# Last sums of a decoder's output: ScalarE scales and stores each block, TensorE adds four ranks, GpSimd two

## The chip, the core and the metric

The kernel runs on one NeuronCore of a Trainium2 chip. The core has five engines with instruction streams of their own, that meet only at semaphores: TensorE (PE in the profile, its weight loads PEld), VectorE (DVE), ScalarE (ACT), GpSimd (POOL) and SyncE (SP), which here only issues DMAs. ScalarE and GpSimd can issue DMAs too. TensorE reads SBUF and writes the eight banks of PSUM; GpSimd does not reach PSUM. The metric is device microseconds of one execution.

## The reference, cut to what matters

Two decoder layers run over 2048 tokens of width 256, each with an attention-like part, a cross attention and a feed-forward part, and a layer norm after each. The change touches only the very last step: the sum of the routed experts' results of a token with what it already has, and the last norm.

```
def _layernorm(x, axis=-1, eps=1e-05):
    m = jnp.mean(x, axis=axis, keepdims=True)
    v = jnp.var(x, axis=axis, keepdims=True)
    return (x - m) / jnp.sqrt(v + eps)
...
    routed = jnp.einsum('te,teh->th', cw, eo)      # six chosen experts of 32 per token
    shared = jax.nn.silu(x @ shared_w_gate) * (x @ shared_w_up) @ shared_w_down
...
    out = routed + shared + ANCHOR_ALPHA * anchor
...
    x = _layernorm(x + _L1_ffn_ref(x, ...), axis=-1)
    return x
```

## The kernel before

All tensors are float32. One large SBUF tensor, `arena`, holds everything; the names in the code are slices of it, and the profile writes "arena" for each of them. The last stage is written by hand, engine by engine, in `tensor_experts`, `scalar_experts`, `vector_experts`, `gpsimd_experts` and `sync_experts`. It has two loops.

The first (`steps_g`) runs over 158 tiles of 128 sorted rows, for 31 of which the anchor experts and for 127 the routed experts are applied. GpSimd scatters each result to its place in the DRAM tensor `yr`, in which the six results of a token stand in a row. VectorE meanwhile adds the anchor results to X.

The second (`steps_i`) is the one in question. It runs over 16 blocks of 128 tokens. SyncE waits for the last scatters and then issues 16 loads (L2221), one per block, each of 128 x 1536 values (768 KB): six ranks of 256 columns per token, into `WB`. Then, in the same queue, come 16 stores (L2224), each behind a wait until its block is scaled. A step n of `steps_i` is "weigh" for block n, "sum" for block n-1 and "scale" for block n-2; an engine takes from this order what belongs to it:

- TensorE, at "weigh": waits for the load of block c and adds ranks 0, 1, 2 by three matmuls with the identity matrix into bank c % 4 (L142 is the line of the helper `mm`). The bank must be free, that is, read by VectorE for block c-4.
- GpSimd, at "weigh": adds ranks 3 and 4 into `tmp3[c % 2]` (L2168). At "sum": (variance + eps) to the power -0.5, 128x1 (L180, in the helper `norm_rstd`).
- VectorE, at "sum": adds rank 5 to X (L2142), then tmp3 (L2145), then the bank (L2148), then the statistics (L167, L170) and the variance (L172). At "scale" for the block before: waits for L180 and for the store that used the same buffer of `xt2_ring` three blocks ago (`o_out`), and writes (x - mean) * rstd there (L187).
- ScalarE does nothing in this loop.

The helper that scales, and the end of SyncE's program:

```
        def norm_scale(v, n, nb, src, dst):
            st = stats[n % 6]
            v.wait_ge(rstd, n + 1)
            for b in range(nb):
                h = v.tensor_scalar(dst(b), src(b), st[:, 24 + 2 * b:25 + 2 * b], st[:, 40 + b:41 + b], ALU.subtract, ALU.mult)
```

`stats` is a ring of six tiles: a block's mean is in column 24, its variance in 32, its rstd in 40.

Of the kernel before, what the change touches and what calls it, by code (L numbers as in the profile page):

```python
# [64 lines left out]
def build(nc, ins, out):  # L65
    with ExitStack() as ctx:
# [1880 lines left out]
        def vector_ends(v, u):  # L1947
# [57 lines left out]
        y2_out = [(s_, 64) for s_ in yg_in]  # L2005
        ag_land = [sem(f"ag_land{i}") for i in range(4)]
        o_out = [sem(f"o_out{i}") for i in range(3)]
        w_copied, silu_done, an_added, added, paired, out_done, tiled, ranked = (
            sem(n) for n in ("w_copied", "silu_done", "an_added", "added", "paired", "out_done", "tiled", "ranked"))
        blocks_in = [(s_, 16) for s_ in x_in + w_in] + [(s_, 64 if i == 0 else 48) for i, s_ in enumerate(taps_in)] + [(s_, 32) for s_ in ctx_in]  # L2010

        def wait_block(e, n):
# [18 lines left out]
        def steps_i():  # L2031
            for n in range(18):
                for u, d in (("weigh", 0), ("sum", 1), ("scale", 2)):
                    if 0 <= n - d < 16:
                        yield u, n - d

        def tensor_experts(t):
            for u, n in steps_g():
# [30 lines left out]
            for u, c in steps_i():  # L2069
                if u == "weigh":  # L2070
                    t.wait_ge(blocks_in[c][0], blocks_in[c][1] + 16)
                    b, k = use(("sum", c), c % 4)
                    t.wait_ge(bank_free[b], k)
                    for kk in range(3):
                        h = mm(t, banks[b][:, 0:256], ident, WB[:, c * 1536 + kk * 256:c * 1536 + kk * 256 + 256], kk == 0, kk == 2)
                    h.then_inc(bank_full[b], 1)

        def scalar_experts(a):
            a.wait_ge(tiled, 1)
            for u, n in steps_g():  # L2080
                I = 64 if n < NTA else 128
                if u == "wl" and n % 2:
                    load_anchor(a, n)
                elif u == "tr" and I == 128:
                    if n >= 3:
                        b, k = U["gu", n - 3]
                        a.wait_ge(bank_full[b], k + 1)
                    b, k = U["tr1", n]
                    a.wait_ge(bank_full[b], k + 1)
                    a.activation(xt2_ring[n % 3], banks[b][:, 0:256], ACT.Copy).then_inc(bank_free[b], 1)  # L2090
                elif u == "gu":
                    if n >= 3:
                        b, k = U["dn", n - 3]
                        a.wait_ge(bank_full[b], k + 1)
                    b, k = U["gu", n]
                    a.wait_ge(bank_full[b], k + 1)
                    a.activation(h2_ring[n % 3][0:I, 0:128], banks[b][0:I, 0:128], ACT.Silu).then_inc(silu_done, 1)  # L2097
                elif u == "dn":
                    if n >= NY:
                        wait_result(a, n - NY)  # L2100
                    b, k = U["dn", n]
                    a.wait_ge(bank_full[b], k + 1)
                    a.activation(y2_ring[n % NY], banks[b][:, 0:256], ACT.Copy, scale=x2_ring[n % NX][:, 257:258]).then_inc(bank_free[b], 1)  # L2103

        def vector_experts(v):
            for u, n in steps_g():
# [30 lines left out]
            for u, c in steps_i():  # L2137
                xx = xblock(c)
                if u == "sum":
                    b, k = U["sum", c]  # L2140
                    v.wait_ge(blocks_in[c][0], blocks_in[c][1] + 16)
                    v.tensor_tensor(xx, WB[:, c * 1536 + 1280:c * 1536 + 1536], xx, ALU.add).then_inc(added, 1)  # L2142
                    v.wait_ge(added, 3 * c + 1)
                    v.wait_ge(paired, c + 1)
                    v.tensor_tensor(xx, tmp3[c % 2], xx, ALU.add).then_inc(added, 1)  # L2145
                    v.wait_ge(added, 3 * c + 2)
                    v.wait_ge(bank_full[b], k + 1)
                    v.tensor_tensor(xx, banks[b][:, 0:256], xx, ALU.add).then_inc(bank_free[b], 1)  # L2148
                    v.wait_ge(bank_free[b], k + 1)
                    held[c] = norm_stats(v, 1, lambda i: xx)  # L2150
                    v.engine_nop().then_inc(added, 1)
                elif u == "scale":
                    if c >= 3:
                        v.wait_ge(o_out[c % 3], 16 * (c // 3))
                    norm_scale(v, held[c], 1, lambda i: xx, lambda i: xt2_ring[c % 3]).then_inc(out_done, 1)

        def gpsimd_experts(p):
            for u, n in steps_g():
# [4 lines left out]
            for u, c in steps_i():  # L2163
                if u == "weigh":
                    if c >= 2:
                        p.wait_ge(added, 3 * (c - 2) + 2)
                    p.wait_ge(blocks_in[c][0], blocks_in[c][1] + 16)
                    p.tensor_tensor(tmp3[c % 2], WB[:, c * 1536 + 768:c * 1536 + 1024], WB[:, c * 1536 + 1024:c * 1536 + 1280], ALU.add).then_inc(paired, 1)  # L2168
                elif u == "sum":
                    norm_rstd(p, 1)  # L2170

# [8 lines left out]
        def sync_experts(s):  # L2180
# [38 lines left out]
            s.wait_ge(w_copied, NT1)  # L2219
            for c in range(16):  # L2220
                s.dma_start(WB[:, c * 1536:(c + 1) * 1536], yr[c * 768:(c + 1) * 768, :].rearrange("(p k) f -> p (k f)", k=6)).then_inc(blocks_in[c][0], 16)  # L2221
            for c in range(16):
                s.wait_ge(out_done, c + 1)
                s.dma_start(out[c * 128:(c + 1) * 128, :], xt2_ring[c % 3]).then_inc(o_out[c % 3], 16)  # L2224
            for j in range(3):
                s.wait_ge(o_out[j], 16 * len(range(j, 16, 3)))

# [158 lines left out]
```

## Time and profile before

| | us |
|---|---|
| median of 3 runs (lowest, highest) | 1797.25 (1795.85, 1801.81) |
| the profiled execution | 1799.82 |
| its span, first to last instruction | 1797.9 |
| the last scatter issued by GpSimd | 1730.1 |
| first and last of the 16 loads issued | 1732.3, 1744.3 |
| last scaling (L187) begins | 1793.5 |

### The profile page before, as it was taken

The page shows a single profiled execution, that of the slowest core. Times are in us where ns is not written, and L with a number is a line of the kernel's source. Part 1 is how long each engine was busy: PE and PEld are TensorE (multiplying, and loading weights), DVE is VectorE, ACT ScalarE, POOL GpSimd, SP SyncE. Part 2 cuts the span into 40 slices and gives each one's busy share as a digit, 9 for nine tenths or more (in the row PEclk, how much of TensorE's full clock was granted, in tenths as well). Part 3 has the DMA queues.
Part 4 walks back from the last instruction along what each step waited for, and adds up shares of the span by engine and source line. Part 5 has one row for each costly group of instructions (what it writes and reads, how often), then busy time and mean ns, then how long its engine had stood idle before and what let it go on. Part 6 is the DMA issues. An engine that isn't in the chain of part 4 may idle for free.

```text
span 1797.9 us, 29185 instructions
## 1 busy us (share of the span) xinstructions
PE 1498.5 (83%) x10012; PEld 1132.1 (63%) x10012; DVE 924.0 (51%) x2506; ACT 538.5 (30%) x1375; POOL 506.9 (28%) x505
## 2 busy tenths in 40 slices
PE   7668987399999998359997798888876799999972
PEld 3455766289999997135674466565653467888862
DVE  7363555511121112897753457585776222666655
ACT  4204443112222221001111254343441112666630
POOL 2020100111111102432222111343344522665653
PEclk9999998599999998679999899999987855999987
DMA  7860000298989982100000511122346664555543
GB/s 211 219 219 25 1 26 13 79 395 326 323 326 329 332 320 83 50 24 0 1 1 1 167 53 42 53 83 83 104 135 223 216 200 143 169 167 158 155 190 150
DMA packets 135088, 260.48 MB, mean 145 GB/s; under 512 B 13727, under 2 KB 107835, under 8 KB 128672
## 3 DMA queue, kind: packets, MB, share of 16 engines
q1 hardware_dynamic: 116032, 214.82, 35.6%
q0 software_dynamic: 16752, 39.88, 6.4%
q10 hardware_dynamic: 2160, 3.93, 0.7%
q8 instruction: 82, 1.34, 0.3%
q14 instruction: 62, 0.51, 0.1%
HBM read 197.31 MB, written 52.59 MB: 139 GB/s over the span
## 4 chain that ended last, share of the span: by engine, by line
PE 51%; DVE 12%; issue 8%; POOL 5%; DMA 3%; ACT 1%; SPq 0%; POOLq 0%; DVEq 0%; ACTq 0%
PE bank L142 47%; POOL xe L1544 3%; PE bank L2045 2%; DVE arena L167 1%; DVE arena L187 1%; DMA out_x<-arena 1%; DMA arena<-xe 1%; DVE arena L1362 1%; POOL arena L1270 1%; DVE arena L1823 1%; POOL arena L180 1%; PE bank L1052 1%; DVE arena L1813 1%; DMA arena<-xd,arena 0%; DVE arena L170 0%
## 5 line engine op out<-in xcount | busy, mean ns | idle before, releaser
L142 PE MATMUL bank<-arena 128*128 128x128 f32 (+9 forms) x8686 | 1351.1, 341 | 181.5 <-issue 25.5
L142 PEld LDWEIGHTS bank<-arena 128*128 128x128 f32 (+5 forms) x8686 | 990.3, 183 | 495.1 <-issue 323.0
L2162 POOL DMA_INDIRECT yr<-arena x158 | 160.0, 1013 | 157.3 <-ACT arena L2103 98.7
L180 POOL TENSOR_TENSOR arena<-arena 128x1 f32<-128x1 f32 (+1 forms) x64 | 54.4, 851 | 521.1 <-DVE arena L172 521.0
L1085 DVE TENSOR_SCALAR arena<-bank,arena 128x128 f32<-128x128 f32 x188 | 52.9, 344 | 272.3 <-PE bank L142 272.3
L1104 POOL DMA_INDIRECT arena<-xd,arena x47 | 44.6, 950 | 295.1 <-PE bank L1052 261.2
L1544 POOL DMA_INDIRECT xe<-arena x112 | 112.4, 1003 | 47.2 <-issue 31.0
L2123 DVE COPY arena<-arena 128x768 f32 x127 | 71.6, 564 | 64.9 <-issue 64.9
L2103 ACT ACTIVATE arena<-bank,arena 128x256 f32<-128x256 f32 x158 | 75.0, 474 | 54.1 <-PE bank L142 48.0
L1725 ACT ACTIVATE arena<-bank,arena 128x256 f32<-128x256 f32 x128 | 59.0, 473 | 98.4 <-DVE arena L1813 98.4
L1072 ACT ACTIVATE arena<-bank,arena 128x128 f32<-128x128 f32 x188 | 53.8, 368 | 90.1 <-PE bank L142 90.1
L2097 ACT ACTIVATE arena<-bank 128x128 f32<-128x128 f32 (+1 forms) x158 | 43.7, 276 | 118.9 <-PE bank L142 118.9
L1063 ACT ACTIVATE arena<-bank 128x256 f32<-128x256 f32 x47 | 18.1, 384 | 201.3 <-PE bank L142 201.3
L2045 PE MATMUL bank<-arena 128*128 128x128 f32 x316 | 69.2, 305 | 9.3 <-DMA arena<-xe 9.2
L187 DVE TENSOR_SCALAR arena<-arena 128x256 f32<-128x256 f32 x160 | 62.0, 438 | 25.3 <-DMA out_x<-arena 14.8
L167 DVE BATCH_NORM_STATS2 arena<-arena 128x6 f32<-128x256 f32 x160 | 58.6, 416 | 2.4
L2131 DVE TENSOR_TENSOR arena<-bank,arena 128x128 f32<-128x128 f32 (+1 forms) x158 | 45.9, 290 | 26.9 <-ACT arena L2097 10.3
L745 DVE TENSOR_REDUCE arena<-bank 128x4 f32<-128x512 f32 x64 | 39.8, 685 | 37.8 <-PE bank L142 37.8
L1251 ACT ACTIVATE arena<-bank 128x512 f32<-128x512 f32 x32 | 19.1, 597 | 123.6 <-PE bank L142 98.1
L1765 POOL TENSOR_TENSOR arena<-arena 128x512 f32<-128x512 f32 x16 | 20.2, 1265 | 118.7 <-DVE arena L1804 118.7
L2045 PEld LDWEIGHTS bank<-arena 128*128 128x128 f32 x316 | 40.9, 153 | 19.3 <-DMA arena<-xe 10.5
L2114 DVE COPY arena<-bank 128x256 f32<-128x256 f32 x31 | 13.2, 424 | 76.3 <-PE bank L2045 76.3
(241 smaller groups left out, 1343.7 us busy)
## 6 DMA issues: line engine op xcount, KB each, us to landing
arena<-in_bank SPq DMA_DIRECT2D x47, 2052.0 KB
arena<-xe SPq DMA_DIRECT2D x158, 129.0 KB, 2.1
arena<-kd SPq DMA_DIRECT2D x16, 1024.0 KB, 11.0
arena<-arena SPq DMA_DIRECT2D x16, 896.0 KB, 4.5
arena<-in_bank SPq DMA_DIRECT2D x8, 1536.0 KB, 11.3
arena<-yr SPq DMA_DIRECT2D x16, 768.0 KB, 14.6
xe<-arena SPq DMA_DIRECT2D x1, 6321.0 KB, 26.1
ys<-arena SPq DMA_DIRECT2D x47, 128.0 KB, 3.2
```

Source lines behind the costliest of these rows:

```text
L142: return t.matmul(o, l, r, start=start, stop=stop, skip_group_check=True)
L167: h = v.bn_stats(st[:, 6 * b:6 * b + 6], src(b)).then_inc(vstep.up(), 1)
L180: p.tensor_tensor(st[:, 40:40 + nb], st[:, 32:32 + nb], cc("mhalf", 0, nb), ALU.pow).then_inc(rstd, 1)
L187: h = v.tensor_scalar(dst(b), src(b), st[:, 24 + 2 * b:25 + 2 * b], st[:, 40 + b:41 + b], ALU.subtract, ALU.mult)
L1072: h = a.activation(h_ring[i % 3][:, m * 128:(m + 1) * 128], banks[b][:, m * 128:(m + 1) * 128], ACT.Relu, bias=sbc(w_ring[i % 5], 4096 + m))
L1085: h = v.tensor_scalar(h_ring[i % 3][:, (4 + m) * 128:(5 + m) * 128], banks[b][:, m * 128:(m + 1) * 128], sbc(w_ring[i % 5], 4100 + m), 0.0 ...
L1544: p.indirect_dma_start(xe, bass.IndirectOffsetOnAxis(ap=posi[i][:, at:at + 1], axis=0), stg[i][:, at * RW:(at + 1) * RW], None).then_inc(a ...
L1725: h = a.activation(f_s[g % 2][:, hh * 512 + j * 256:hh * 512 + j * 256 + 256], banks[b][:, j * 256:j * 256 + 256], ACT.Exp, scale=-1.0, bi ...
L2045: h = t.transpose(banks[b][:, j * 128:(j + 1) * 128], x2_ring[n % NX][:, j * 128:(j + 1) * 128], ident)
L2103: a.activation(y2_ring[n % NY], banks[b][:, 0:256], ACT.Copy, scale=x2_ring[n % NX][:, 257:258]).then_inc(bank_free[b], 1)
L2123: v.tensor_copy(e_ring[n % 4], WB[:, bass.ds(at * ROW1, ROW1)]).then_inc(w_copied, 1)
L2162: p.indirect_dma_start(yr, bass.IndirectOffsetOnAxis(ap=sidx.bitcast(I32)[:, n:n + 1], axis=0), y2_ring[n % NY], None, bounds_check=14335, ...
```

## The change

Four things in the second loop:

1. TensorE adds four ranks (0 to 3) instead of three, and GpSimd adds ranks 4 and 5 instead of 3 and 4. VectorE's addition of the sixth rank (L2142) goes, with its wait for the load.
2. VectorE no longer scales. At "scale" it computes only the shift, -mean * rstd, 128x1.
3. ScalarE scales from X into `xt2_ring` with an Identity activation (scale rstd, bias shift), after waiting for the shift and for the buffer's old store. It waits for its own activation and issues the store from its own queue. SyncE's sixteen stores go.
4. VectorE waits before the statistics of block c until ScalarE has scaled block c-6, whose tile of `stats` they overwrite. One empty instruction per block goes.

```
@@ tensor_experts
-                    for kk in range(3):
-                        h = mm(t, banks[b][:, 0:256], ident, WB[:, c * 1536 + kk * 256:c * 1536 + kk * 256 + 256], kk == 0, kk == 2)
+                    for kk in range(4):
+                        h = mm(t, banks[b][:, 0:256], ident, WB[:, c * 1536 + kk * 256:c * 1536 + kk * 256 + 256], kk == 0, kk == 3)
@@ scalar_experts
+            for c in range(16):
+                st = stats[(NORMS + c) % 6]
+                a.wait_ge(shifted, c + 1)
+                if c >= 3:
+                    a.wait_ge(o_out[c % 3], 16 * (c // 3))
+                a.activation(xt2_ring[c % 3], xblock(c), ACT.Identity, scale=st[:, 40:41], bias=shift[:, c:c + 1]).then_inc(scaled, 1)
+                a.wait_ge(scaled, c + 1)
+                a.dma_start(out[c * 128:(c + 1) * 128, :], xt2_ring[c % 3]).then_inc(o_out[c % 3], 16)
@@ vector_experts, "sum"
-                    v.wait_ge(blocks_in[c][0], blocks_in[c][1] + 16)
-                    v.tensor_tensor(xx, WB[:, c * 1536 + 1280:c * 1536 + 1536], xx, ALU.add).then_inc(added, 1)
-                    v.wait_ge(added, 3 * c + 1)
                     v.wait_ge(paired, c + 1)
                     v.tensor_tensor(xx, tmp3[c % 2], xx, ALU.add).then_inc(added, 1)
-                    v.wait_ge(added, 3 * c + 2)
+                    v.wait_ge(added, c + 1)
                     v.wait_ge(bank_full[b], k + 1)
                     v.tensor_tensor(xx, banks[b][:, 0:256], xx, ALU.add).then_inc(bank_free[b], 1)
                     v.wait_ge(bank_free[b], k + 1)
+                    if c >= 6:
+                        v.wait_ge(scaled, c - 5)
                     held[c] = norm_stats(v, 1, lambda i: xx)
-                    v.engine_nop().then_inc(added, 1)
@@ vector_experts, "scale"
-                    if c >= 3:
-                        v.wait_ge(o_out[c % 3], 16 * (c // 3))
-                    norm_scale(v, held[c], 1, lambda i: xx, lambda i: xt2_ring[c % 3]).then_inc(out_done, 1)
+                    st = stats[held[c] % 6]
+                    v.wait_ge(rstd, held[c] + 1)
+                    v.scalar_tensor_tensor(shift[:, c:c + 1], st[:, 24:25], -1.0, st[:, 40:41], ALU.mult, ALU.mult).then_inc(shifted, 1)
@@ gpsimd_experts, "weigh"
-                    p.tensor_tensor(tmp3[c % 2], WB[:, c * 1536 + 768:c * 1536 + 1024], WB[:, c * 1536 + 1024:c * 1536 + 1280], ALU.add).then_inc(paired, 1)
+                    p.tensor_tensor(tmp3[c % 2], WB[:, c * 1536 + 1024:c * 1536 + 1280], WB[:, c * 1536 + 1280:c * 1536 + 1536], ALU.add).then_inc(paired, 1)
@@ sync_experts
-            for c in range(16):
-                s.wait_ge(out_done, c + 1)
-                s.dma_start(out[c * 128:(c + 1) * 128, :], xt2_ring[c % 3]).then_inc(o_out[c % 3], 16)
```

The order on VectorE in the middle of the second loop, before: the empty instruction (ISA), the scaling of a block (L187), then the six instructions of the next sum.

```order
L2151 ISA
L187 TENSOR_SCALAR arena<-arena 128x256
L2142 TENSOR_TENSOR arena<-arena 128x256
L2145 TENSOR_TENSOR arena<-arena 128x256
L2148 TENSOR_TENSOR arena<-bank,arena 128x256
L167 BN_STATS arena<-arena 128x6
L170 BN_AGGR arena<-arena 128x2
L172 TENSOR_SCALAR arena<-arena 128x1
```

The same place after; L2155 is the line of the old L2145, L2158 that of L2148, L2167 the shift.

```order
L2167 SCALAR_TENSOR_TENSOR arena<-arena 128x1
L2155 TENSOR_TENSOR arena<-arena 128x256
L2158 TENSOR_TENSOR arena<-bank,arena 128x256
L167 BN_STATS arena<-arena 128x6
L170 BN_AGGR arena<-arena 128x2
L172 TENSOR_SCALAR arena<-arena 128x1
```

Of seven working instructions per block five wide or statistic ones stay, and the scaling has become an instruction on one column.

The end of ScalarE's program before, from the last tiles of the first loop (L2097 Silu, L2103 the weighted results) to its last branch:

```order
L2097 ACTIVATE arena<-bank 128x128
L2103 ACTIVATE arena<-bank,arena 128x256
L2097 ACTIVATE arena<-bank 128x128
L2103 ACTIVATE arena<-bank,arena 128x256 x2
L66 UNCONDITIONAL_BRANCH
```

And after (L2101 and L2107 are the same two lines), where the pair L2114, L2116 stands sixteen times:

```order
L2101 ACTIVATE arena<-bank 128x128
L2107 ACTIVATE arena<-bank,arena 128x256 x2
L2114 ACTIVATE arena<-arena 128x256
L2116 DMA out_x<-arena 128x256
L2114 ACTIVATE arena<-arena 128x256
L2116 DMA out_x<-arena 128x256
```

The stores have moved from SyncE's queue, where they stood behind all sixteen loads, to ScalarE's, where each stands behind the scaling of its block. All that comes before the second loop stands as it did on every engine.

## Rows read from the trace of the kernel before

**Rows 1.** VectorE's timeline, one block: start, duration, instruction, [idle before <-releaser]

```profile
1765.42 0.41 DVE L187 TENSOR_SCALAR arena<-arena 128x256 f32<-128x256 f32 x1 [14.85 <-DMA out_x<-arena]
1765.74 0.42 DVE L2142 TENSOR_TENSOR arena<-arena 128x256 f32<-128x256 f32 x1
1766.20 0.42 DVE L2145 TENSOR_TENSOR arena<-arena 128x256 f32<-128x256 f32 x1
1766.66 0.42 DVE L2148 TENSOR_TENSOR arena<-bank,arena 128x256 f32<-128x256 f32 x1
1767.12 0.43 DVE L167 BATCH_NORM_STATS2 arena<-arena 128x6 f32<-128x256 f32 x1
1767.58 0.18 DVE L170 BATCH_NORM_AGGREGATE arena<-arena 128x2 f32<-128x6 f32 x1
1767.80 0.15 DVE L172 TENSOR_SCALAR arena<-arena 128x1 f32<-128x1 f32 x1
1767.88 0.41 DVE L187 TENSOR_SCALAR arena<-arena 128x256 f32<-128x256 f32 x1
```

**Rows 2.** SyncE's issues of loads (last two, all) and stores: ns min/median/max, landing

```profile
L2221 SPq DMA_DIRECT2D arena<-yr x2: 1578/1578/1579, 1742.7 to 1744.3; - x2
DMA to landing us min/median/max: 20.5/20.6/20.7
...
L2221 SPq DMA_DIRECT2D arena<-yr x16: 331/450/3646, 1732.3 to 1744.3; - x16
...
L2224 SPq DMA_DIRECT2D out_x<-arena x16: 332/332/1604, 1745.9 to 1793.9; - x16
...
DMA to landing us min/median/max: 1.7/1.7/19.5
```

**Rows 3.** Windows: length, busy and (count) per engine, PEclk, DMA share, GB/s

```profile
1450.00:1460.00 10.00, 10.00 (x35) 6.57 (x34) 1.94 (x7) 2.24 (x6) 2.88 (x3) 0.50 0.47 135
...
1746.00:1748.00 2.00, 1.56 (x6) 1.06 (x6) 1.83 (x6) 0.00 (x0) 1.37 (x2) 1.00 1.01 418
...
1774.00:1775.00 1.00, 0.37 (x2) 0.38 (x3) 0.90 (x4) 0.00 (x0) 0.60 (x1) 1.00 0.39 131
```

**Rows 4.** Timelines of TensorE's first sums, and VectorE's first read of a bank

```profile
1736.57 3.36 PE L142 MATMUL bank<-arena 128*128 128x256 f32 x7 [8.07 <-DMA arena<-yr]
...
1739.60 0.42 DVE L2148 TENSOR_TENSOR arena<-bank,arena 128x256 f32<-128x256 f32 x1 [1.54 <-PE bank L142]
...
1741.64 2.54 PE L142 MATMUL bank<-arena 128*128 128x256 f32 x11
...
1746.20 1.56 PE L142 MATMUL bank<-arena 128*128 128x256 f32 x6 [0.33 <-DMA arena<-yr]
```

**Rows 5.** Timeline: GpSimd's last pair and last power, VectorE's last scaling

```profile
1788.39 1.00 POOL L2168 TENSOR_TENSOR arena<-arena 128x256 f32<-128x256 f32 x1
...
1792.68 0.67 POOL L180 TENSOR_TENSOR arena<-arena 128x1 f32<-128x1 f32 x1 [1.80 <-DVE arena L172]
...
1793.46 0.41 DVE L187 TENSOR_SCALAR arena<-arena 128x256 f32<-128x256 f32 x1 [0.51 <-POOL arena L180]
```

**Rows 6.** ScalarE: activations (busy, mean ns), its DMA issues: 1400 to 1440, alone

```profile
L2103 ACT ACTIVATE arena<-bank,arena 128x256 f32<-128x256 f32 x158 | 75.0, 474 | 54.1 <-PE bank L142 48.0
...
L339 ACT ACTIVATE arena<-arena 128x512 f32<-128x512 f32 x8 | 4.5, 620 | 0.0
...
L2178 ACTq DMA_DIRECT2D arena<-in_banka x7: 344/345/397, 1400.0 to 1438.4; - x7
...
DMA to landing us min/median/max: 2.9/5.4/8.1
...
DMA to landing us min/median/max: 2.6/2.6/2.6
```

**Rows 7.** SyncE's timeline in the first expert stage: two stores, one tile apart

```profile
404.55 0.33 SPq L1114 DMA_DIRECT2D ys<-arena  x1
...
411.80 0.33 SPq L1114 DMA_DIRECT2D ys<-arena  x1
```

More of the change, by code:

```diff
@@ L2007, in build @@
         o_out = [sem(f"o_out{i}") for i in range(3)]
-        w_copied, silu_done, an_added, added, paired, out_done, tiled, ranked = (
-            sem(n) for n in ("w_copied", "silu_done", "an_added", "added", "paired", "out_done", "tiled", "ranked"))
+        w_copied, silu_done, an_added, added, paired, tiled, ranked = (
+            sem(n) for n in ("w_copied", "silu_done", "an_added", "added", "paired", "tiled", "ranked"))
         blocks_in = [(s_, 16) for s_ in x_in + w_in] + [(s_, 64 if i == 0 else 48) for i, s_ in enumerate(taps_in)] + [(s_, 32) for s_ in ctx_in]
@@ L2035, in steps_i @@
                         yield u, n - d
+        NORMS = 48
+        shift = alloc(16)
+        shifted, scaled = sem("shifted"), sem("scaled")
         def tensor_experts(t):
@@ L2149, in vector_experts @@
                     v.wait_ge(bank_free[b], k + 1)
+                    if c >= 6:
+                        v.wait_ge(scaled, c - 5)
                     held[c] = norm_stats(v, 1, lambda i: xx)
-                    v.engine_nop().then_inc(added, 1)
+                    assert held[c] == NORMS + c
                 elif u == "scale":
-                    if c >= 3:
-                        v.wait_ge(o_out[c % 3], 16 * (c // 3))
-                    norm_scale(v, held[c], 1, lambda i: xx, lambda i: xt2_ring[c % 3]).then_inc(out_done, 1)
+                    st = stats[held[c] % 6]
+                    v.wait_ge(rstd, held[c] + 1)
+                    v.scalar_tensor_tensor(shift[:, c:c + 1], st[:, 24:25], -1.0, st[:, 40:41], ALU.mult, ALU.mult).then_inc(shifted, 1)
         def gpsimd_experts(p):
@@ L2165, in gpsimd_experts @@
                     if c >= 2:
-                        p.wait_ge(added, 3 * (c - 2) + 2)
+                        p.wait_ge(added, c - 1)
                     p.wait_ge(blocks_in[c][0], blocks_in[c][1] + 16)
-                    p.tensor_tensor(tmp3[c % 2], WB[:, c * 1536 + 768:c * 1536 + 1024], WB[:, c * 1536 + 1024:c * 1536 + 1280], ALU.add).then_inc(paired, 1)
+                    p.tensor_tensor(tmp3[c % 2], WB[:, c * 1536 + 1024:c * 1536 + 1280], WB[:, c * 1536 + 1280:c * 1536 + 1536], ALU.add).then_inc(paired, 1)
                 elif u == "sum":
```

## The prediction, made before the changed kernel ran

> **What bounds the kernel now.** I read VectorE's waits in the last 70 us first, then its timeline. One wait stands out: 14.85 us in front of L187, the scaling of a block, for a store to out_x [rows 1]. Nothing else there costs more than two microseconds on the engine that carries the chain. The list of DMA issues says why [rows 2]: the stores were issued on SyncE behind the sixteen loads of WB. The last load was issued at 1744.3 and landed 20.5 us later, at 1764.8; the first store, issued at 1745.9, took 19.5 us and landed at 1765.4, where an undisturbed one takes 1.7. L187 writes into a ring of three buffers, so the scaling of block 3 had to wait for store 0, and with it everything behind it on VectorE.
>
> The windows show the loads as a stream at the limit of the DMA engines: share 1.01 at 418 GB/s [rows 3], and so until 1764, so 768 KB every 1.88 us. After the stall VectorE is the bound: its timeline shows seven working instructions a block without a gap, 1765.42 to 1767.88, 2.46 us each [rows 1]. Eleven sums (blocks 5 to 15) were still to do: 11 x 2.46 = 27.1 us from 1765.7, then 5.1 us of tail. So the end of the kernel has two parts that do not overlap: a stream of loads (to 1764.8) and a backlog on VectorE. The best that a change of this stage can do is to make the sums keep up with the loads, and to end soon after the last one lands.
>
> **The change part by part**, on the profiled execution's clock (its span is 1797.9, the execution 1799.82 us, 2.6 above the median of 1797.25).
>
> *VectorE.* L2142 goes (start to start 0.46 in [rows 1]) and L187 goes (0.33). The new 128x1 instruction is not in this trace; the nearest is L172 with the same shape, 0.15 busy and 0.08 to the next start [rows 1]. I take 0.15, with 0.08 and 0.33 (that of the wide L187) as ends. A block is then 2.46 - 0.46 - 0.33 + 0.15 = 1.82 us (1.75 to 2.0). That is just under the 1.88 us between loads, so VectorE no longer falls behind.
>
> *TensorE.* Four matmuls instead of three. At the granted clock of 1.00 (2.4 GHz) eleven records take 2.54 us, two records to a matmul: (2.54 - 0.38) / 10 = 0.216 per record, 0.43 per matmul [rows 4]. A block of six records takes 1.56 with its tail; the block's turn grows from about 1.40 to 1.83 us. It also stays under 1.88. Block 0 meets the low level: seven records in 3.36 us there, 0.86 per matmul [rows 4], so the first sum reaches VectorE 0.86 later, at 1740.45 instead of 1739.60 [rows 4]. Later blocks absorb this, because four banks let TensorE run ahead and the loads set the pace. At the end the fourth matmul lies on the path once: 0.43.
>
> *GpSimd.* The pair is another pair, at the same 1.00 us [rows 5]; with the 0.67 of the power a block costs it 1.67, under the load. No term.
>
> *ScalarE* idled through this stage. An activation 128x256 cost 0.47 from PSUM [rows 6]; one of double the width from the arena took 0.62. I take 0.47, with 0.35 and 0.62 as ends. It issues the store itself: issuing on its queue cost 0.345 [rows 6]. A turn is about 0.9 us, under 1.88. Identity was already used among the Silus without a table load in between, so I price none. What stands behind the new wait on o_out is only ScalarE's own next block; VectorE follows through the wait on scaled, six blocks behind.
>
> *SyncE* loses sixteen issues that come after its loads. That frees nothing by itself.
>
> *The stores in the middle of the loads.* This is the term that decides. First the cost to the loads: a lone store of 128 KB occupied 0.39 of one microsecond of all engines, at 131 GB/s [rows 3]. The trace has no store beside this stream, so it leaves bounds: nothing at all (if it hides), and 1.1 us. The upper one comes from the first expert stage, where a 2052 KB load of weights, a 128 KB store and a gather share 7.25 us per tile (404.55 to 411.80) [rows 7]; 2052 KB at 418 GB/s are 5.03, and half of the 2.2 left over is 1.1 per small transfer. I take 0.39, since it is the same transfer.
>
> Second, how soon such a store lands. On ScalarE's own queue, 256 KB landed 2.6 us after issue with nothing around it, and in 2.9 to 8.1 us, median 5.4, in the stretch where SyncE's bulk loads were in flight [rows 6]. So it is held up, but not always until the end of the bulk. I take the top of that, 8 us, because here the stream never pauses; 4 and 12 are the ends I carry.
>
> The Trainium skill, DMA: Bandwidth & Descriptors, section Queues, rings and completion order, says that each DMA engine goes round the queues it has work for, one packet at a time; its section Issuing engines are not separate DMA queues says that issuing from several engines at once only saves the issuing time. By the first rule the stores slip in between the loads, which is my case; by the second, read strictly, nothing is gained but issue time, and that is the first rival below. The 8.1 us row lies between the two.
>
> *The sum.* Block 0 is scaled at about 1744.8 (1740.45, then VectorE's 1.3 for it, then block 1's sum, which stands ahead of block 0's shift in the order). With 8 us per store and three buffers, ScalarE hands over three blocks per 8.5 us: block 3 at 1753.3, block 6 at 1761.9, block 9 at 1770.3. VectorE needs block 9's scaling only for block 15, and is there at about the same time, so it does not stall. Seven stores or so have passed before the last load lands: 1764.8 + 7 x 0.39 = 1767.5. After that stores land in 1.7 us again and ScalarE works off blocks 10 to 15 at 0.87 each (0.47 + 0.35 + 0.05): 1770.3 + 6 x 0.87 = 1775.5. Then 0.05 + 1.7 for the last store and 2.3 to close, as now (L187 at 1793.46 [rows 5], stored from 1793.9, landed 1795.6, end 1797.9): **1779.6**.
>
> With stores that land in 4 us, ScalarE is never late, and the path is the other one: twelve stores pass, the last load lands at 1764.8 + 12 x 0.39 = 1769.5; TensorE 2.0 to 1771.5; VectorE 0.46 + 0.46 + 0.22 + 0.15 to 1772.8; GpSimd 0.05 + 0.67 to 1773.5; shift 0.2, ScalarE 0.52, to 1774.2; then the same 4.05: 1778.3. With 12 us: 1781. The three lie close, since a slower store means fewer of them in front of the last load. With the ends of the store's cost: nothing gives 1775, 1.1 us gives 1784 to 1788. Forecast: span 1779.5, 18.4 less, and from the median 1797.25 - 18.4 = **1779 us**.
>
> **The rivals.**
>
> *Stores wait for all loads.* If the engines finish what SyncE has queued before they touch ScalarE's queue, stores 0 to 2 land at about 1765.8, block 3 is scaled at 1766.4, and VectorE, six blocks ahead at most, has stood at block 9. It then has six more sums at 1.82 and the tail: its block 9 is normed at 1767.4, and 1767.4 + 6 x 1.82 + 1.4 + 4.0 = 1784, a time of 1783. For it: the 19.5 us of store 0 [rows 2], and the slow end of [rows 6]. Against: the median of 5.4 in the same row, and those 19.5 us were on one queue. It is still a gain, since VectorE gets to block 9 instead of block 5, at 1.82 per block.
>
> *TensorE stays at 1.2 GHz.* 64 matmuls x 0.86 = 55 us from 1736.6 to 1791.4, then 3.1 for the last block's norm and scaling and 4.0 to the end: 1798.5, a time of 1798, no change. For it: from 1450 to 1460 it was busy for all 10.00 us and still granted 0.50 [rows 3]. Against: on these same matmuls, the clock rose 4.8 us after they began, and stayed at 1.00 with 1.56 busy of 2.00 [rows 3, 4]; now it is busier.
>
> *ScalarE's issue blocks* (the slower side). SyncE's own issue once took 3.65 us and others 1.6 while its loads were queued [rows 2]. ScalarE runs in order: if every one of its issues took 3.65, a turn would be 4.12 and sixteen of them would end at 1744.8 + 65.9 = 1810.7, with 4.0 behind: 1814.7, a time of 1814. It turns into a loss from (1797.9 - 4.0 - 1744.8) / 16 = 3.07 per turn, an issue of 2.6 us. Against: 0.397 was the longest of seven issues on its queue beside bulk loads [rows 6], and after 1768 the queues are empty.
>
> *The moved store changes nothing*, that is, some other wait as long as the old one takes its place, within 0.3%: I see none, and leave it a small chance.
>
> **How the numbers follow.** The forecast (stores land among the loads, 1775 to 1788) 0.78; stores wait for all loads 0.13; TensorE at 1.2 GHz 0.03; issue blocks 0.03; another wait in its place 0.03. A measurement of this kernel can tell about 0.3% (5.4 us) from no change. Faster: 0.78 + 0.13 = 0.91; same 0.06; slower 0.03. The range runs from 1774 (a store costs the loads nothing, landing fast: 1775, less one for the scatter of the runs) to 1787 (1.1 us per store; it takes in the first rival).
>
> **What the profile after would show.** The wait of VectorE on out_x is gone, and none over 3 us has come in its place before block 15. The last load lands at 1767 to 1770. VectorE's blocks are 1.8 us while it works and end before 1773. ScalarE's stores land in 4 to 12 us before 1768 and 1.7 after it. If they all land after 1765, the first rival holds; if TensorE shows 0.50 beyond 1745, the second; if ScalarE's issues are longer than 1 us, the third. The forecast is wrong if a store beside the loads costs them more than 1.1 us, or if VectorE's block is not 1.8.

## The result, and the profile after

| us | before | after |
|---|---|---|
| median of 4 runs each, side by side | 1796.7 (1795.85 to 1801.81) | 1778.5 (1776.0 to 1781.1) |
| ratio, 95% interval | | 0.9893 (0.9867 to 0.9919) |
| span of the profiled execution | 1797.9 | 1778.5 |
| first load of the last stage issued | 1732.3 | 1733.9 |
| from there to the end ("the stage") | 65.6 | 44.6 |

1779 was predicted, from 1774 to 1787. The two executions reached the last stage 1.6 us apart; within it 21 us are gone. Later executions reached it anywhere from 1718.6 to 1731.2, whatever the kernel (the last section shows where that arises), so from here on the measure is the stage: from the issue of the first of the sixteen loads to the last instruction. Two executions of the changed kernel gave 44.6 and 44.2 by it. Each stage below is of one profiled execution. One of seven runs of a kernel below (in place, stores by ScalarE) took 2274.6 us at a mean granted clock of 0.633, and the median given for it leaves that run out.

VectorE's timeline of the kernel after, one block from the middle of the loads (start, duration, instruction); it answers to [rows 1]:

```profile
1752.68 0.15 DVE L2167 SCALAR_TENSOR_TENSOR arena<-arena 128x1 f32<-128x1 f32 x1
1752.75 0.42 DVE L2155 TENSOR_TENSOR arena<-arena 128x256 f32<-128x256 f32 x1
1753.20 0.42 DVE L2158 TENSOR_TENSOR arena<-bank,arena 128x256 f32<-128x256 f32 x1
1753.66 0.43 DVE L167 BATCH_NORM_STATS2 arena<-arena 128x6 f32<-128x256 f32 x1
1754.12 0.18 DVE L170 BATCH_NORM_AGGREGATE arena<-arena 128x2 f32<-128x6 f32 x1
1754.34 0.15 DVE L172 TENSOR_SCALAR arena<-arena 128x1 f32<-128x1 f32 x1
1754.41 0.15 DVE L2167 SCALAR_TENSOR_TENSOR arena<-arena 128x1 f32<-128x1 f32 x1
```

A block takes 1754.41 - 1752.68 = 1.73 us, in the very stretch in which VectorE stood still before. Behind the 2.61 us that it waits for TensorE in block 0, its longest wait in the loop is now 0.94 us, for TensorE in block 1.

ScalarE's timeline after. The three groups are the first blocks, blocks 3 to 6 in the middle of the loads, and the last three:

```profile
1745.96 0.60 ACT L2114 ACTIVATE arena<-arena 128x256 f32<-128x256 f32 x1 [15.34 <-DVE arena L2167]
1746.59 0.36 ACTq L2116 DMA_DIRECT2D out_x<-arena  x1
...
1753.74 0.60 ACT L2114 ACTIVATE arena<-arena 128x256 f32<-128x256 f32 x1 [3.73 <-DMA out_x<-arena]
1754.37 0.34 ACTq L2116 DMA_DIRECT2D out_x<-arena  x1
1755.92 0.60 ACT L2114 ACTIVATE arena<-arena 128x256 f32<-128x256 f32 x1 [1.57 <-DMA out_x<-arena]
...
1761.15 0.60 ACT L2114 ACTIVATE arena<-arena 128x256 f32<-128x256 f32 x1 [2.46 <-DMA out_x<-arena]
...
1773.64 0.60 ACT L2114 ACTIVATE arena<-arena 128x256 f32<-128x256 f32 x1 [0.76 <-DVE arena L2167]
1774.27 0.34 ACTq L2116 DMA_DIRECT2D out_x<-arena  x1
1774.71 0.60 ACT L2114 ACTIVATE arena<-arena 128x256 f32<-128x256 f32 x1 [0.47 <-ACT arena L2114]
1775.34 0.34 ACTq L2116 DMA_DIRECT2D out_x<-arena  x1
1775.78 0.60 ACT L2114 ACTIVATE arena<-arena 128x256 f32<-128x256 f32 x1 [0.47 <-ACT arena L2114]
1776.41 0.34 ACTq L2116 DMA_DIRECT2D out_x<-arena  x1
```

The wait for a store has not gone: it has moved to ScalarE, 14.3 us over seven blocks, where it costs VectorE nothing. It is still on the path: the chain of work that ended last runs over three stores in turn, of 7.5, 6.7 and 6.1 us. Block 3 is scaled at 1753.74, as soon as store 0, issued at 1746.59, has landed 7.1 us later, still in the middle of the loads. At the end ScalarE works off its backlog in turns of 1.07 us.

The landing times of all sixteen stores, and of the last two loads (minimum, median, maximum); they answer to [rows 2]:

```profile
L2116 ACTq DMA_DIRECT2D out_x<-arena x16: 338/338/363, 1746.6 to 1776.4; - x16
...
DMA to landing us min/median/max: 1.7/5.0/8.0
...
L2233 SPq DMA_DIRECT2D arena<-yr x2: 1578/1578/1579, 1744.0 to 1745.6; - x2
...
DMA to landing us min/median/max: 23.0/23.3/23.6
```

The last load landed at 1745.6 + 23.6 = 1769.2, 35.3 us into the stage; before it landed at 1744.3 + 20.7 = 1765.0, 32.7 into it, with no store landed yet. After, seven stores had landed by then and an eighth was on its way: 2.6 / 8 = 0.33 us of delay for each.

The windows after (columns as in [rows 3]): TensorE's clock is at 1.00 from 1744 on, and with loads and stores together the DMA engines stay at their limit, a share of 1.01 to 1.03.

```profile
1742.00:1744.00 2.00, 2.00 (x7) 1.59 (x7) 1.52 (x5) 0.00 (x0) 0.62 (x1) 0.64 1.01 424
1744.00:1746.00 2.00, 2.00 (x11) 1.76 (x10) 1.33 (x6) 0.04 (x1) 0.82 (x3) 1.00 1.03 430
1752.00:1754.00 2.00, 2.00 (x11) 1.75 (x10) 1.86 (x7) 0.26 (x1) 1.70 (x3) 1.00 1.01 411
```

### The profile page after: what moved, and what is told of

Its sections match the earlier page's. It is cut to its first block, busy times and chain, and to the rows that moved or that the text cites. A ratio compares the mean times of both kernels' runs of the same rounds, so it can differ in the third digit from the quotient of the medians.

```text
span 1778.5 us, 29227 instructions
## 1 busy us (share of the span) xinstructions
PE 1505.8 (85%) x10044; PEld 1140.6 (64%) x10044; DVE 912.9 (51%) x2490; ACT 548.1 (31%) x1391; POOL 506.7 (28%) x505
## 3 DMA queue, kind: packets, MB, share of 16 engines
q1 hardware_dynamic: 113728, 212.72, 35.5%
## 4 chain that ended last, share of the span: by engine, by line
PE 48%; DVE 14%; issue 8%; POOL 6%; DMA 3%; ACT 1%; SPq 0%; POOLq 0%; ACTq 0%; DVEq 0%
PE bank L142 44%; POOL xe L1544 3%; PE bank L2049 2%; DVE arena L1362 2%; DVE arena L167 1%; DVE arena L187 1%; DMA out_x<-arena 1%; DMA arena<-xe 1%; DVE arena L1353 1%; POOL arena L1287 1%; POOL arena L1270 1%; POOL arena L180 1%; DVE arena L1823 1%; DVE arena L1342 1%; PE bank L1052 1%
## 5 line engine op out<-in xcount | busy, mean ns | idle before, releaser
L142 PE MATMUL bank<-arena 128*128 128x128 f32 (+7 forms) x8718 | 1357.2, 341 | 163.3 <-issue 25.1
L1104 POOL DMA_INDIRECT arena<-xd,arena x47 | 44.7, 951 | 295.3 <-PE bank L1052 261.5
L2107 ACT ACTIVATE arena<-bank,arena 128x256 f32<-128x256 f32 x158 | 75.0, 474 | 54.2 <-PE bank L142 48.1
L2101 ACT ACTIVATE arena<-bank 128x128 f32<-128x128 f32 (+1 forms) x158 | 43.7, 276 | 118.2 <-PE bank L142 118.2
L745 DVE TENSOR_REDUCE arena<-bank 128x4 f32<-128x512 f32 x64 | 39.7, 684 | 37.7 <-PE bank L142 37.7
L187 DVE TENSOR_SCALAR arena<-arena 128x256 f32<-128x256 f32 x144 | 53.9, 430 | 10.0 <-POOL arena L180 9.6
```

Source lines behind the costliest of these rows:

```text
L142: return t.matmul(o, l, r, start=start, stop=stop, skip_group_check=True)
```

## The experiments

The change is three things at once: shorter sums on VectorE, a scaling that VectorE need not wait for, and stores in a queue of their own. The theory: the stall of 14.85 us came from three buffers together with a store that stood behind all loads, and the shorter sums were worth the rest. The rivals: the queue is everything; the queue is nothing but issue time.

**Part one alone: four ranks.** The kernel before, with only this:

```
-                    for kk in range(3):
+                    for kk in range(4):
...
-                    v.tensor_tensor(xx, WB[:, c * 1536 + 1280:c * 1536 + 1536], xx, ALU.add).then_inc(added, 1)
...
-                    p.tensor_tensor(tmp3[c % 2], WB[:, c * 1536 + 768:c * 1536 + 1024], WB[:, c * 1536 + 1024:c * 1536 + 1280], ALU.add).then_inc(paired, 1)
+                    p.tensor_tensor(tmp3[c % 2], WB[:, c * 1536 + 1024:c * 1536 + 1280], WB[:, c * 1536 + 1280:c * 1536 + 1536], ALU.add).then_inc(paired, 1)
```

> The kernel before with the first part of the change alone: four ranks on TensorE, ranks 4 and 5 on GpSimd, L2142 gone; VectorE still scales and SyncE still stores. My theory: the stall for store 0 stays (VectorE waits until the loads have ended), and then eleven blocks take 2.46 - 0.46 = 2.00 us: stage (first load's issue to the last instruction) 65.5 - 5.1 = 60.4 us. Rival, TensorE's fourth matmul becomes the bound, above all at its lower clock after the stall: 63 to 66. Rival, the shorter sums were the main part of the gain: under 55.

Measured: stage 60.4 us; time 1793.7 against 1798.6, ratio 0.9972 (0.9949 to 0.9995). VectorE's longest wait (instruction, what it waited for; total us, count, longest):

```profile
DVE arena L187 <- DMA out_x<-arena: 15.7, 1, 15.7
```

VectorE's timeline of this kernel behind it:

```profile
1761.60 0.41 DVE L187 TENSOR_SCALAR arena<-arena 128x256 f32<-128x256 f32 x1
1761.92 0.42 DVE L2142 TENSOR_TENSOR arena<-arena 128x256 f32<-128x256 f32 x1
...
1763.60 0.41 DVE L187 TENSOR_SCALAR arena<-arena 128x256 f32<-128x256 f32 x1
```

The stall is there in full, 0.9 longer since VectorE reached it sooner; behind it a block takes 2.00 us. The four ranks alone are worth 5.2 of the 21 us, which is the eleven blocks behind the stall at 0.46 each. TensorE was no bound: behind its first bank (2.6 us) VectorE never waited for it.

**The queue alone.** The kernel before, but the stores are issued by ScalarE:

```
@@ scalar_experts
+            for c in range(16):
+                a.wait_ge(out_done, c + 1)
+                a.dma_start(out[c * 128:(c + 1) * 128, :], xt2_ring[c % 3]).then_inc(o_out[c % 3], 16)
@@ sync_experts
-            for c in range(16):
-                s.wait_ge(out_done, c + 1)
-                s.dma_start(out[c * 128:(c + 1) * 128, :], xt2_ring[c % 3]).then_inc(o_out[c % 3], 16)
```

> The kernel before with one thing changed: the sixteen stores are issued by ScalarE instead of SyncE; VectorE still scales. The last stage is timed from the issue of the first of the sixteen loads to the last instruction: 65.6 us in the kernel before (1732.3 to 1797.9), 44.6 in the changed one (1733.9 to 1778.5). My theory: the stall of 14.85 us goes, but stores among the loads land in 7 to 8 us, as after the change, and VectorE's own scaling now waits for the three buffers: about 2.7 us per block until the loads end, then 2.46. Stage 51 to 54 us, 12 to 14 less than before. Rival, the queue is the whole gain: 44 to 46. Rival, another queue saves only issue time: 64 to 66.

Measured: stage 52.1 us; time 1783.0 against 1796.9, ratio 0.9932 (0.9907 to 0.9957). The size was right, the way to it not quite. VectorE's wait for the buffers:

```profile
DVE arena L187 <- DMA out_x<-arena: 0.5, 1, 0.5
```

The landing times of its sixteen stores:

```profile
DMA to landing us min/median/max: 1.7/5.7/7.5
```

VectorE's timeline of this kernel, the scalings of two blocks in a row:

```profile
1751.21 0.41 DVE L187 TENSOR_SCALAR arena<-arena 128x256 f32<-128x256 f32 x1
...
1753.67 0.41 DVE L187 TENSOR_SCALAR arena<-arena 128x256 f32<-128x256 f32 x1
```

I had expected 2.7 us per block from the buffers; VectorE was held by them for 0.5 us in all, and took its own 2.46 per block. Three blocks of 2.46 are 7.4, just about what a store needs. So the queue alone is worth 13.5 us, and what stays is VectorE's length per block.

**All but the queue.** The changed kernel with the stores back on SyncE:

```
@@ scalar_experts
-                a.wait_ge(scaled, c + 1)
-                a.dma_start(out[c * 128:(c + 1) * 128, :], xt2_ring[c % 3]).then_inc(o_out[c % 3], 16)
@@ sync_experts
+            for c in range(16):
+                s.wait_ge(scaled, c + 1)
+                s.dma_start(out[c * 128:(c + 1) * 128, :], xt2_ring[c % 3]).then_inc(o_out[c % 3], 16)
```

> The changed kernel with its stores back on SyncE's queue, behind the sixteen loads; all else as changed. My theory: stores 0 to 2 land only when the loads have ended (about 33.5 us into the stage), ScalarE is held at block 3 and VectorE at block 9 (it needs the scaling of block 3), then six more blocks at 1.73 and the tail: stage 51 to 52 us, 7 more than the changed kernel and 14 less than before. Rival, ScalarE's own queue gave nothing but issue time: 45. Rival, the queue is the whole gain: 64 to 66.

Measured: stage 50.4 us; time 1781.8 against 1796.9, ratio 0.9925 (0.9902 to 0.9948). Its waits:

```profile
ACT arena L2114 <- DMA out_x<-arena: 19.7, 4, 17.2
...
DVE arena L167 <- ACT arena L2114: 9.1, 1, 9.1
```

This is the first rival of the prediction, built on purpose. ScalarE stands 17.2 us at block 3, and VectorE 9.1 us once, at the statistics of the block that needs that scaling. The stage is 6.0 us longer than with the stores on their own queue. So the queue is worth 13.5 us without the rest and 6.0 with it, since VectorE, six blocks ahead instead of three buffers, is hurt less by the same stall.

**No wait for a buffer, and no store among the loads.** ScalarE scales in place in X, where the block has its own room, and SyncE stores behind its loads:

```
-                if c >= 3:
-                    a.wait_ge(o_out[c % 3], 16 * (c // 3))
-                a.activation(xt2_ring[c % 3], xblock(c), ACT.Identity, scale=st[:, 40:41], bias=shift[:, c:c + 1]).then_inc(scaled, 1)
-                a.wait_ge(scaled, c + 1)
-                a.dma_start(out[c * 128:(c + 1) * 128, :], xt2_ring[c % 3]).then_inc(o_out[c % 3], 16)
+                a.activation(xblock(c), xblock(c), ACT.Identity, scale=st[:, 40:41], bias=shift[:, c:c + 1]).then_inc(scaled, 1)
@@ sync_experts
+            for c in range(16):
+                s.wait_ge(scaled, c + 1)
+                s.dma_start(out[c * 128:(c + 1) * 128, :], xblock(c)).then_inc(o_out[c % 3], 16)
```

> The changed kernel, but ScalarE scales in place in X (sixteen buffers, so no wait for a store), and SyncE issues the stores behind its loads. No store then takes time from a load. My theory: the loads end 32.5 us into the stage, as before the change; TensorE's last block starts at 32.6, GpSimd's last power at 36.1, and the end comes 5.2 after that by GpSimd's closing drain (5.03 us in the kernel before), where the last store alone would allow 39.7: stage 41.3 us, 3.3 less than the changed kernel. Rival, that drain does not set the end: 39.7. Rival, the gain needs the stores on their own queue: 51 or more, as with the stores on SyncE and three buffers.

Measured: stage 41.8 us (median 1775.8 beside 1796.9). It was run a second time beside the changed kernel:

> In-place scaling with the stores on SyncE behind the loads, again: stage 41.8 us, 2.8 less than the changed kernel; time 1775 to 1776 against 1778.5.

> The changed kernel once more, beside the three below: stage (first load's issue to the last instruction) 44.6 us.

Measured there: 41.8 us against 44.2. The very queue that made the stall is the better one as soon as nobody waits for the buffers: it holds the stores back by itself until the loads are through, and the last load landed 33.1 and 33.2 us into the stage, not 35.3 and 35.5. In whole times the two could not be told apart (medians 1774.7 and 1774.4 of six runs each, before 1795.6).

**In place, but stores among the loads.** The changed kernel, scaling in X; the stores stay with ScalarE:

```
-                if c >= 3:
-                    a.wait_ge(o_out[c % 3], 16 * (c // 3))
-                a.activation(xt2_ring[c % 3], xblock(c), ACT.Identity, scale=st[:, 40:41], bias=shift[:, c:c + 1]).then_inc(scaled, 1)
+                a.activation(xblock(c), xblock(c), ACT.Identity, scale=st[:, 40:41], bias=shift[:, c:c + 1]).then_inc(scaled, 1)
...
-                a.dma_start(out[c * 128:(c + 1) * 128, :], xt2_ring[c % 3]).then_inc(o_out[c % 3], 16)
+                a.dma_start(out[c * 128:(c + 1) * 128, :], xblock(c)).then_inc(o_out[c % 3], 16)
```

> The changed kernel with in-place scaling (sixteen buffers), stores still issued by ScalarE among the loads. In the changed kernel the three buffers held ScalarE back to the end (its last scaling 2.5 us after the last shift). My theory: that hold goes, but nine to eleven stores instead of seven now pass ahead of the last load, which lands 0.7 later, and GpSimd's closing drain, 5.2 us after the last power, takes over as the end: stage 44.7 us, no gain. Rival, the three buffers alone are the end: 42 to 43. Rival, the in-place kernel of the last batch got its 41.8 us from the buffers and not from the queue: 41.8 here too.

Measured: stage 44.2 us (median 1777.0 beside 1795.6), no gain over the changed kernel. ScalarE's backlog was shorter (its last activation began 40.2 us into the stage instead of 41.5 in the changed kernel beside it), but the loads ended no sooner, and the last store was no longer the end: it had landed at 1773.1, 1.7 us before the kernel ended. What ended last was GpSimd's closing, as the next experiment shows. It is the pair with the kernel above that tells: the same buffers, another queue, 2.4 us.

**What closes the kernel.** In the kernel before, 2.3 us lie between the landing of the last store and the end. The closing instructions of the queues (L66) of the kernel before (times in ns, minimum, median and maximum, then the start):

```profile
L66 POOLq DRAIN  x1: 5026/5026/5026, 1792.6 to 1792.6; - x1
```

and of the kernel after:

```profile
L66 POOLq DRAIN  x1: 4901/4901/4901, 1772.7 to 1772.7; - x1
```

To test it, the in-place kernel with SyncE's stores, but without GpSimd's last power; VectorE copies the variance in its place, so block 15 is not normed:

```
-                elif u == "sum":
+                elif u == "sum" and c < 15:
                     norm_rstd(p, 1)
@@ vector_experts
+                    if c == 15:
...
+                        v.tensor_scalar(st[:, 40:41], st[:, 32:33], 1.0, None, ALU.mult).then_inc(vstep.up(), 1)
```

> As the in-place kernel with stores on SyncE, but GpSimd leaves out its last power, that of block 15: VectorE copies the variance in its place (block 15 of the output is not normed rightly), so that GpSimd's last work is about 2 us earlier. If GpSimd's closing drain sets the end of the in-place kernel, the stage falls from 41.3 to about 39.3 and is then set by the last store. If the drain is no bound, only the 0.5 us that the copy is shorter than the power are seen, from 39.7 to 39.2.

Measured: stage 39.9 us, 1.9 less; with the drain as no bound only 0.5 was to be had. Then the same without leaving anything out (ROOTS is 14):

```
@@ scalar_experts, before the loop
+            a.activation(early[:, 0:1], cc("ones", 0, 1), ACT.Sqrt)
@@ in the loop, before the scaling of block c
+                if c + 1 >= ROOTS and c + 1 < 16:
+                    s1 = stats[(NORMS + c + 1) % 6]
+                    a.wait_ge(variance, NORMS + c + 2)
+                    a.activation(s1[:, 33:34], s1[:, 32:33], ACT.Sqrt).then_inc(rooted, 1)
@@ vector_experts, "scale"
-                    v.wait_ge(rstd, held[c] + 1)
+                    if c < ROOTS:
+                        v.wait_ge(rstd, held[c] + 1)
+                    else:
+                        v.wait_ge(rooted, c - ROOTS + 1)
+                        v.reciprocal(st[:, 40:41], st[:, 33:34]).then_inc(inverted, 1)
+                        v.wait_ge(inverted, c - ROOTS + 1)
@@ gpsimd_experts
-                elif u == "sum":
+                elif u == "sum" and c < ROOTS:
```

> The in-place kernel with stores on SyncE, in which the last two of the sixteen powers move from GpSimd to ScalarE (square root, with its table loaded while ScalarE is idle) and VectorE (reciprocal). Nothing is left out. GpSimd's last power is then that of block 13 and its last work the pair of block 15. If the closing drain set the end, the stage falls from 41.8 to 39.5 to 40 us (the last store then sets it). If moving work off GpSimd at the end does nothing, 41.5 to 42.

The first activation is there so that the table of the root is loaded while ScalarE is idle: the load stands at 1722.96 in this trace and takes 1.28 us. Measured: stage 40.1 us; median 1772.7 against 1795.6, ratio 0.9887 (0.9848 to 0.9927). The issue of the first load on SyncE's timeline of this kernel:

```profile
1726.21 13.45 SPq L2242 DMA_DIRECT2D arena<-yr  x16
```

Its span is 1766.3 us. The closing drain of its GpSimd:

```profile
L66 POOLq DRAIN  x1: 5687/5687/5687, 1759.4 to 1759.4; - x1
```

The drain now ends at 1765.1, 1.2 us before the end. The last store landed 39.8 us into the stage in the in-place kernel, 39.5 without the last power and 39.7 here, so what shortened the stage by 1.9 and 1.7 us was the drain. It is recorded as 5.7 us here, since the power of block 13 and the pair of block 15 fall into it; it ends 4.3 us behind the end of that pair (1760.79), as it does behind the last power elsewhere. By the stage this version beats both kernels, the changed one by 4.1 us; its whole time lies below the changed one's of the same set (1774.4) by less than the scatter.

**The term in dispute, doubled.** The changed kernel with each block stored twice, once to another tensor:

```
+                a.dma_start(extra[c * 128:(c + 1) * 128, :], xblock(c)).then_inc(x_out, 16)
                 a.dma_start(out[c * 128:(c + 1) * 128, :], xt2_ring[c % 3]).then_inc(o_out[c % 3], 16)
```

> The changed kernel, with every block stored twice: ScalarE first stores the unscaled block to another DRAM tensor, then the scaled one to the output. This doubles the one term in dispute, what a store among the loads costs them. In the changed kernel the last load's data ended 34.6 to 34.8 us into the stage with 8.5 to 8.8 stores in front, against 32.3 with one or two: 0.32 us per store. If the cost is linear and ScalarE's queue gets its turn as before, some 16 to 18 stores pass and the last load ends at 37 to 37.7; the stage is 47 to 49 us (44.4 plus 2.6 for the loads, and up to 2 for the queue of the doubled stores). If the queue takes a fixed share of the engines however much is queued, 34.8 and a stage over 49. If stores beside loads grow dearer (1.1 us each), over 42 and a stage over 51.

Measured: stage 52.1 us, time 1783.5 against 1798.6. The landing times of its stores to the output, to the extra tensor, and of the loads, in this order:

```profile
DMA to landing us min/median/max: 1.8/2.0/13.7
...
DMA to landing us min/median/max: 1.7/1.7/11.9
...
DMA to landing us min/median/max: 4.2/14.8/24.8
```

The expectation's second variant holds, that the queue takes a fixed share. Twice as many stores were ready, but when the last load landed, 35.8 us into the stage (1739.1 + 24.1 - 1727.4; 35.3 and 35.5 with single stores), only nine had landed and a tenth was on its way, where it had been seven and an eighth. What grew is the time that a store waits, up to 13.7 us instead of 8.0. ScalarE, held by its buffers, then had nine blocks to go instead of six, each about 1.5 us instead of 1.07: that, and not the loads, is most of what the stage is longer. From the first landing on the nine came over 18 us, one for each load. The packets of the two queues of the changed kernel in its stage, the loads' first (packets, MB, share of the 16 engines):

```profile
q1 hardware_dynamic: 2304, 12.58, 66.6%
q10 hardware_dynamic: 2304, 2.10, 13.4%
```

A load and a store have the same number of packets. If the engines take as many from one queue as from the other in turn, one store passes per load and costs it the time of its bytes, by my estimate 128 / 768 x 1.88 = 0.31 us, which fits the 0.33 measured; no run varied the packets to test this. The Trainium skill says in DMA: Bandwidth & Descriptors, section Queues, rings and completion order, that the engines go round the queues packet by packet; this agrees. What the Trainium skill says there in section Issuing engines are not separate DMA queues, that issuing from several engines only saves issue time, does not fit the 13.5 us of the queue alone here. Why the first store took 7.1 us with no other store before it stays open.

The stages side by side (us):

| kernel | expected | measured |
|---|---|---|
| before | | 65.6 |
| four ranks alone | 60.4 | 60.4 |
| queue alone | 51 to 54 | 52.1 |
| all but the queue | 51 to 52 | 50.4 |
| changed kernel | 47.2 (1779.5 - 1732.3) | 44.6, 44.2 |
| in place, ScalarE stores | 44.7 | 44.2 |
| in place, SyncE stores | 41.3 | 41.8, 41.8 |
| in place, SyncE stores, last power left out | 39.3 | 39.9 |
| in place, SyncE stores, last two powers as roots | 39.5 to 40 | 40.1 |
| every block stored twice | 47 to 49, or over 49 | 52.1 |

## Why the prediction was right, point by point

- **The bound.** Right: a stream of loads, then a backlog on VectorE, held up by store 0. The two partial kernels show both halves at their size: 13.5 us for the queue, 5.2 for the four ranks. The last load was read a little early: its landing was the 20.7 of [rows 2], not 20.5.
- **VectorE.** 1.82 was forecast for a block, 1.73 measured: the shift costs 0.07 from start to start, the lower end that I had given, as L172 does beside its follower.
- **TensorE.** 0.86 later in block 0: the first read of a bank came 8.11 us into the stage instead of 7.27, 0.84 later. Afterwards VectorE waited for it 0.94 us at most, and in the last blocks TensorE was itself waiting for loads. The rival's sum has a slip: 1736.6 + 55 is 1791.6, not 1791.4.
- **GpSimd.** No term, right, but the price was off: the pair took 0.73, not 1.00 (last section).
- **Landing of the stores.** 8 us taken; 7.1, 7.5 and 8.0 for the first three, 6 to 7 for the next. Of the three values carried, the one from the top of the range of other transfers came nearest.
- **Cost to the loads.** 0.39 taken for each of seven stores, 0.33 measured for each of eight; the last load landed 35.3 us into the stage, where I had it at 1767.5 - 1732.3 = 35.2.
- **ScalarE.** 0.47 for the activation, which took 0.60 from SBUF; a turn was 1.07 instead of 0.87. The row of L339, from the arena, was the nearer one and I had put it at the end of the range. Two errors met here: since the stores landed in 6 to 7 us, the scaling of block 9 ended 35.2 us into the stage, where I had 38.0, but the six turns behind it took 7.3 us instead of 5.2. The last activation ended at 42.5 instead of 43.2.
- **The close.** "2.3 to close, as now" is the step that failed. It was read off the kernel before as if it were a fixed cost behind the last store. It was GpSimd's drain, running beside the store; after the change 0.4 us are left. This term was too large by 1.9.
- **The sum.** The stage lost 21 us, where 18.4 were forecast: 1.9 of the difference come from the close, 0.7 from ScalarE. The medians differ by 18.2; that they match the forecast so closely is luck to the extent of those 2.6 us: the changed kernel's profiled execution reached the stage 1.6 us later, and two executions of that same kernel differ by 13.5 us there (last section).
- **Rivals.** Stores behind all loads: not so, and its price was good: a stage of 51.4 forecast (1783.7 - 1732.3), 50.4 measured where the case was built. TensorE at 1.2 GHz throughout: no, it was granted 1.00 from 1744 on. ScalarE's issues never took more than 0.36 us, while SyncE's still took up to 3.4 beside its own backlog.

## What to carry to other kernels

A store that is queued behind a bulk of loads lands after them; that hurts only through the buffers that wait for it. Before moving it to another queue, ask whether the buffers can be had, since the old queue then keeps the stores out of the loads' way for free. What lies between the last landing and the end of a kernel is not a constant: look for the engine whose closing drain ends last, and see that its last work ends earlier, by giving the last small operation to another engine.

## What the runs showed of the hardware that I had not expected

**GpSimd's closing drain** ended 4.3 us behind the end of GpSimd's last work in all twelve profiled executions, whether that was a power (0.55 to 0.73 us) or, with the last powers moved, the pair. Its record runs from 4.9 to 5.7 us, since it starts before that work ends. It was the last to end in the kernel before and in five of the experiments: the four ranks alone, the queue alone, all but the queue, and both in-place kernels with all powers.

**GpSimd's addition beside VectorE's.** The pair took a median of 997 ns before and 726 after, and 721 in the kernel with four ranks alone. Before:

```profile
L2168 POOL TENSOR_TENSOR arena<-arena x16: 717/997/1002, 1736.6 to 1788.4; 128x256 f32<-128x256 f32 x16
```

After:

```profile
L2180 POOL TENSOR_TENSOR arena<-arena x16: 713/726/728, 1738.1 to 1769.3; 128x256 f32<-128x256 f32 x16
```

Four ranks alone:

```profile
L2165 POOL TENSOR_TENSOR arena<-arena x16: 716/721/727, 1722.9 to 1770.4; 128x256 f32<-128x256 f32 x16
```

Before, it began with an addition of two SBUF tensors on VectorE (1768.67 beside L2145 at 1768.66) and was 0.28 longer: in twelve of the sixteen blocks it began so and took 0.996 to 1.002 us, in the other four 0.717 to 0.722. In block 0 the pair was the first, at 1736.60, and VectorE's addition of two SBUF tensors came 0.02 us behind it; there the pair took 0.72, and the addition 0.98 instead of 0.42:

```profile
1736.62 0.98 DVE L2142 TENSOR_TENSOR arena<-arena 128x256 f32<-128x256 f32 x1 [8.87 <-DMA arena<-yr]
```

So of the two that began together, the later one was delayed. The Trainium skill, SBUF — State Buffer, section Who interferes with whom, says that such a VectorE instruction and a GpSimd instruction that reads SBUF hold each other up; the rows agree, though no run was made for this alone.

**The time ahead of the stage.** The two executions of the changed kernel reached the last stage at 1733.9 and 1720.4, 13.5 us apart, and the kernel before at 1732.3. The windows show where. The kernel before, 1480 to 1530 (PEclk is the third value from the end):

```profile
1480.00:1530.00 50.00, 50.00 (x198) 35.17 (x197) 13.93 (x47) 15.11 (x41) 15.53 (x16) 0.57 0.47 140
```

The second execution of the kernel after, the same stretch:

```profile
1480.00:1530.00 50.00, 48.97 (x275) 36.84 (x276) 20.82 (x69) 21.91 (x60) 21.81 (x22) 0.82 0.59 177
```

In the 50 us ahead of that, both were granted 0.50 with TensorE busy throughout; one was back at 2.4 GHz from 1500 on and had 275 matmul records in the window, the other only from 1530 on (0.85 from 1520 to 1530), with 198. At 2.4 GHz, 50 us hold 368 records in the kernel before (1530 to 1580), so by my estimate the 77 missing ones are 10.5 us, most of the 12 between these two. The first execution of the kernel after had 0.55, like the kernel before, so it is not the change. What decides when the clock rises there stays open. Where a change moves some microseconds at the end of such a kernel, the stage has to be timed by itself.
